# Gate rows spread by DMA, GpSimd's aggregates behind VectorE's first, buffers and prologue order changed

## The reference

```
h    = gelu(gelu(cond @ W0 + b0) @ W1 + b1);  att = softmax(h @ W2 + b2)     # 32 x 8, once
aggw = sum_k att[t, k] * weight[k]  (128 x 128);  aggb = att[t] @ bias_k
y    = bf16(aggw @ x[t] + aggb)
qg, sg = quant(y * inv_gate);  qu, su = quant(y * inv_up)     # per row: scale = max|.| / 127, codes = round
gate = (qg @ w_gate.T) * sg * s_wgate;  up = (qu @ w_up.T) * su * s_wup      # 1024 columns
inter = bf16(clip(silu(gate) * up, -10, 10));  qi, si = quant(inter * inv_inter)
out[t] = x[t] + (qi @ w_down.T) * si * s_wdown
```

## Time and profile before

| | us |
|---|---|
| median of 3 runs | 838.83 (838.81 to 840.03) |
| the profiled execution | 838.61 |
| its span, first instruction to last | 836.8 |
| PE busy | 811.7 |
| DVE busy | 715.6 |
| ACT busy | 443.0 |
| POOL busy | 152.1 |

### The profile page before, as it was taken

The page is one execution under the profiler, slowest core; times in us unless marked ns, Lnnn a source line. Parts: engine busy times, 40 slices in busy tenths (PEclk is TensorE's granted clock), DMA queues, the critical chain, the costliest instruction groups (busy, mean ns, idle before and its releaser), DMA issues.

```text
span 836.8 us, 9194 instructions
## 1 busy us (share of the span) xinstructions
PE 811.7 (97%) x3531; PEld 365.9 (44%) x3531; DVE 715.6 (86%) x799; ACT 443.0 (53%) x379; POOL 152.1 (18%) x146
## 2 busy tenths in 40 slices
PE   7898969899999999999999999999999999999997
PEld 2344434344444444444444444444444444444443
DVE  5575847999888898888889988888898888889968
ACT  2767322566565555565555556555555565545541
POOL 5630002111222222012222210222221012222000
PEclk9999989999999999999999999999999999999999
DMA  9962534355445454444554544445454454554242
GB/s 272 216 149 51 101 101 169 104 159 160 113 151 164 139 164 139 117 140 120 164 160 142 141 136 139 113 151 163 139 162 141 119 132 127 164 157 145 89 113 101
DMA packets 157918, 117.72 MB, mean 141 GB/s; under 512 B 147497, under 2 KB 147625, under 8 KB 148274
## 3 DMA queue, kind: packets, MB, share of 16 engines
q1 hardware_dynamic: 156146, 104.55, 41.4%
q0 software_dynamic: 1728, 12.58, 7.5%
HBM read 59.44 MB, written 33.55 MB: 111 GB/s over the span
## 4 chain that ended last, share of the span: by engine, by line
PE 88%; DVE 6%; ACT 2%; DMA 2%; issue 1%; DVEq 0%; ACTq 0%
PE up_ps L506 24%; PE gate_ps L506 24%; PE down_ps L580 24%; PE conv_ps L453 13%; DVE amax L875 1%; DMA wd<-w_downT 1%; DMA qgT<-qg 1%; PE down_ps L423 1%; DVE region L965 1%; DVE region L971 1%; ACT qg L686 0%; PE up_ps L423 0%; DVE region L981 0%; PE gate_ps L580 0%; PE conv_ps L415 0%
## 5 line engine op out<-in xcount | busy, mean ns | idle before, releaser
L506 PE MATMUL gate_ps<-wg,qgT 128*128 128x512 bf16 x992 | 219.7, 379 | 1.6 <-ACT qgT L730 1.6
L580 PE MATMUL down_ps<-wd,qiT 128*128 128x512 bf16 x912 | 214.8, 379 | 2.1 <-ACT qiT L766 2.1
L506 PE MATMUL up_ps<-wu,quT 128*128 128x512 bf16 x960 | 216.7, 379 | 0.0
L875 DVE TENSOR_REDUCE amax<-region 128x1 f32<-128x2048 f32 (+1 forms) x93 | 178.8, 1923 | 1.3
L357 POOL TENSOR_TENSOR prod<-wexp,att_bc 128x1024 f32<-128x1024 f32 x31 | 58.9, 1901 | 541.6 <-DVE region L915 516.6
L506 PEld LDWEIGHTS gate_ps<-wg,qgT 128*128 128x128 bf16 x992 | 96.9, 98 | 119.4 <-ACT qgT L730 2.1
L580 PEld LDWEIGHTS down_ps<-wd,qiT 128*128 128x128 bf16 x912 | 89.1, 98 | 128.0 <-issue 30.0
L506 PEld LDWEIGHTS up_ps<-wu,quT 128*128 128x128 bf16 x960 | 93.8, 98 | 113.5 <-issue 0.6
L453 PE MATMUL conv_ps<-xt,aggw 128*128 128x512 f32 x256 | 124.7, 612 | 6.1 <-issue 2.9
L686 ACT ACTIVATE qg<-region,recip 128x2048 f16<-128x2048 f32 x30 | 60.1, 2002 | 125.9 <-DVE recip L885 125.9
L677 ACT ACTIVATE y<-conv_ps,aggb 128x512 bf16<-128x512 f32 x120 | 81.8, 686 | 75.4 <-PE conv_ps L453 70.7
(11 more groups left out here) (124 smaller groups left out, 509.3 us busy)
## 6 DMA issues: line engine op xcount, KB each, us to landing
xt<-x SPq DMA_DIRECT2D x32, 1024.0 KB, 4.8
out<-xt SPq DMA_DIRECT2D x31, 1024.0 KB, 4.0
wg<-w_gateT POOLq DMA_DIRECT2D x4, 1024.0 KB, 19.0
wu<-w_upT POOLq DMA_DIRECT2D x4, 1024.0 KB, 19.5
wd<-w_downT POOLq DMA_DIRECT2D x4, 1024.0 KB, 7.7
out<-xt SPq DMA_DIRECT2D x4, 256.0 KB, 2.7
wexp<-weightT SPq DMA_DIRECT2D x1, 512.0 KB, 3.8
qgT<-qg SPq DMA_TRANSPOSE x28, 3.7
```

What stands on the lines that cost most here:

```text
L506: last = nc.tensor.matmul(acc[:, n * BANK:(n + 1) * BANK], codes[:, k * P:(k + 1) * P], wts[:, k, n * BANK:(n + 1) * BANK], start=(k == 0) ...
L580: last = nc.tensor.matmul(down_bank(t, c), qiT_at(t)[:, k * P:(k + 1) * P], wd[:, k, c * BANK:(c + 1) * BANK], start=(k == 0), stop=(k == ...
L875: nc.vector.tensor_reduce(amax[:, i:i + 1], src, axis=AX.X, op=ALU.max, apply_absolute_value=True).then_inc(max_ready, 1)
```

## The change

It does six things.
- inv_gate, inv_up and s_gate come as three inputs, and SP loads each with one DMA that reads the row 128 times, straight into invg_bc, invu_bc and swg_bc. inv_gate stands between x(0) and x(1); the other two follow the late rows, behind a wait for w_gate's third chunk, and x(3) follows them. All `spread` matmuls on TensorE, their ScalarE copies and the `warm` matmuls go.
- GpSimd waits for `agg_step` K (all of VectorE's aggregate of tile 0) before its own first aggregate.
- The scaled gate of tile 1 moves from w_down's part 5 to `prod`; the qiT buffers of tiles 0 and 1 move from `prod` to `qg`. GpSimd's wait for down(1) goes; ScalarE's `quant_g(4)` gets it. `gate_out(1)` waits for the aggregate of tile 4.
- TensorE: turn_u(0) stands before the first half of gate(2), not after it.
- ScalarE: quant_g(1) before conv_out(2); turned_g(2) and turned_u(0) earlier; quant_g(3) before silu(2); quant_u(3) from before turned_g(3) to after turned_i(2).
- VectorE: quant_g(3) before gate_out(2); quant_u(3) from before inner(1) to after inner(2).

```diff
-        GATE_HOME = [down_sc2[:, :], wd_part(5, fp32), wd_part(6, fp32)]
+        GATE_HOME = [down_sc2[:, :], prod[:, :, :].rearrange("p k o -> p (k o)"), wd_part(6, fp32)]
...
-        prod_bf = prod[:, :, :].rearrange("p k o -> p (k o)").bitcast(bf16)
-        QIT_HOME = [prod_bf[:, 0:KI * P], prod_bf[:, KI * P:2 * KI * P]]
+        qg_bf = qg[:, :].bitcast(bf16)
+        QIT_HOME = [qg_bf[:, 0:KI * P], qg_bf[:, KI * P:2 * KI * P]]
...
-            sp.dma_start(invg_s[0], rows[:, 0:I]).then_inc(rows_in[0], 16)
             sp.dma_start(wexp[:, :, :], weightT).then_inc(wexp_in, 16)
-            sp.dma_start(invg_s[1], rows[:, I:2 * I]).then_inc(rows_in[1], 16)
             sp.dma_start(xslot(0), x[0, :, :]).then_inc(x_in[0], 16)
+            sp.dma_start(invg_bc[:, :], inv_gate.partition_broadcast(P)).then_inc(rows_in[INVG], 16)
             sp.dma_start(xslot(1), x[1, :, :]).then_inc(x_in[1], 16)
-            for i, home in enumerate((invu_s[0], invu_s[1], swg_s)):
-                sp.dma_start(home, rows[:, (2 + i) * I:(3 + i) * I]).then_inc(rows_in[2 + i], 16)
             sp.dma_start(xslot(2), x[2, :, :]).then_inc(x_in[2], 16)
             for i, home in enumerate((swu_s, invi_s, swd_s[0], swd_s[1])):
                 sp.dma_start(home, late_rows[:, i * I:(i + 1) * I]).then_inc(late_in[i], 16)
+            sp.wait_ge(wg_in[2], 16)
+            sp.dma_start(invu_bc[:, :], inv_up.partition_broadcast(P)).then_inc(rows_in[INVU], 16)
+            sp.dma_start(swg_bc[:, :], s_gate.partition_broadcast(P)).then_inc(rows_in[SWG], 16)
             sp.wait_ge(gcodes_ready, 2)
...
-            pool.wait_ge(att_dve, ATT - 1)
+            pool.wait_ge(agg_step, K)
             aggregate(1)
...
-            pool.wait_ge(down_done, NC * 2)
...
-            pe.wait_ge(ones_set, 1)
-            warm(9)
             pe.wait_ge(mlp_in, 16)
+            pe.wait_ge(ones_set, 1)
...
-            for u in range(4):
-                spread(u)
-                warm(1)
             conv(0)
-            spread(4)
-            spread(5)
             conv(1)
             turn_g(0)
             conv(2)
             gate(0, HALVES[0])
-            spread(6)
-            spread(7)
             turn_g(1)
             gate(0, HALVES[1])
-            spread(8)
-            spread(9)
             gate(1, HALVES[0])
             turn_g(2)
             gate(1, HALVES[1])
+            turn_u(0)
             gate(2, HALVES[0])
-            turn_u(0)
             conv(3)
...
+                elif t == EARLY + 1:
+                    act.wait_ge(down_done, NC * 2)
...
-            for u in range(4):
-                spread_copy(u)
             conv_out(0)
-            spread_copy(4)
-            spread_copy(5)
             conv_out(1)
             quant_g_first()
             turned_g(0)
+            quant_g(1)
             conv_out(2)
-            quant_g(1)
-            spread_copy(6)
-            spread_copy(7)
             turned_g(1)
             quant_g(2)
-            spread_copy(8)
-            spread_copy(9)
+            turned_g(2)
             quant_u(0)
-            turned_g(2)
+            turned_u(0)
             silu(0)
-            turned_u(0)
             quant_u(1)
             conv_out(3)
             silu(1)
             turned_u(1)
             quant_u(2)
+            quant_g(3)
             silu(2)
-            quant_g(3)
             turned_u(2)
             quant_i(0)
-            quant_u(3)
             turned_g(3)
             turned_i(0)
             quant_i(1)
             turned_i(1)
             quant_i(2)
             turned_i(2)
+            quant_u(3)
             turned_u(3)
...
+                if t == 1:
+                    dve.wait_ge(agg_ready, 4)
...
             quant_u(2)
+            quant_g(3)
             gate_out(2)
-            quant_g(3)
             inner(0)
-            quant_u(3)
             inner(1)
             inner(2)
+            quant_u(3)
```

More of the change, by code:

```diff
@@ L3, with adaln_ffn @@
 from contextlib import ExitStack
-def adaln_ffn(nc, x, mlp, b2, weightT, w_gateT, w_upT, w_downT, rows, late_rows, out):
+def adaln_ffn(nc, x, mlp, b2, weightT, w_gateT, w_upT, w_downT, inv_gate, inv_up, s_gate, late_rows, out):
     fp32 = mybir.dt.float32
@@ L117, in adaln_ffn @@
         qiT16 = qiT[:, :].bitcast(fp16)
-        invg_s = wd_part(0, fp32)[0:1, :], wd_part(1, fp32)[0:1, :]
-        invu_s = wd_part(2, fp32)[0:1, :], wd_part(3, fp32)[0:1, :]
-        swg_s = wd_part(5, fp32)[0:1, :]
         swu_s = quT[0:1, :].bitcast(fp32)
@@ L137, in adaln_ffn @@
         ones = qiT[:, 0:2 * P].bitcast(fp32)
-        warm_s = qiT[:, 0:2 * P]
         logits = region2[:, 768:768 + B * K]
@@ L161, in adaln_ffn @@
         log_ps = up_ps[:, 0:B * K]
-        warm_ps = conv_ps[:, BANK:BANK + 2 * P]
         gturn_ps = down_ps[:, :].bitcast(fp16)
@@ L168, in adaln_ffn @@
         wexp_in = sem("wexp_in")
-        rows_in = [sem(f"rows_in{i}") for i in range(5)]
+        rows_in = [sem(f"rows_in{i}") for i in range(3)]
         late_in = [sem(f"late_in{i}") for i in range(4)]
@@ L182, in adaln_ffn @@
         ident_set = sem("ident_set")
-        spread_mm = sem("spread_mm")
-        spread_out = sem("spread_out")
         gturn_mm = sem("gturn_mm")
@@ L237, in adaln_ffn @@
         result_ready = sem("result_ready")
-        INVG, INVU, SWG = 4, 8, 10
+        INVG, INVU, SWG = range(3)
         SWU, INVI, SWD = 1, 2, 4
@@ L250, in adaln_ffn @@
         last_turn_ps = [bank(up_ps, h).bitcast(fp16)[:, 0:BANK] for h in range(2)]
[L252 to L257, removed]
         def gate_acc(t):
@@ L411, in _ @@
         def _(pe):
[L413 to L424, removed]
+            pe.wait_ge(mlp_in, 16)
             pe.wait_ge(ones_set, 1)
-            warm(9)
-            pe.wait_ge(mlp_in, 16)
             nc.tensor.matmul(hid_ps, w0_s, embT_s, start=True, stop=True).then_inc(hid_mm, 1)
-            warm(1)
             pe.wait_ge(hid_act, 1)
             nc.tensor.matmul(hid_ps, w1_s, h1, start=True, stop=True).then_inc(hid_mm, 1)
-            warm(3)
             pe.wait_ge(att_dve, 1)
@@ L444, in conv @@
                 for c in cs:
-                    if t == 0 and c < 2:
-                        pe.wait_ge(spread_out, 3)
-                    elif t == 3 and c < 2:
+                    if t == 3 and c < 2:
                         pe.wait_ge(uturn_out, c + 1)
@@ L450, in conv @@
                         pe.wait_ge(uturn_out, 9 + c)
-                    else:
+                    elif t > 0 or c >= 2:
                         pe.wait_ge(y_ready, NC * t + c - 1)
@@ L464, in turn_g @@
                     pe.wait_ge(gcodes_half, 1)
-                    pe.wait_ge(spread_out, 6)
                 else:
@@ L513, in gate @@
                         pe.wait_ge(qgT_ready, t - EARLY)
[L514 to L518, removed]
+                    if t == 2:
                         pe.wait_ge(gateval_ready, 1)
@@ L521, in gate @@
                         pe.wait_ge(upval_ready, 2)
-                    else:
+                    elif t > EARLY:
                         pe.wait_ge(gateval_ready, t)
@@ L659, in _ @@
         def _(act):
-            def spread_copy(u):
-                act.wait_ge(spread_mm, u + 1)
-                nc.scalar.activation(SPREAD_INTO[u], SPREAD_BANK[u], ACT.Copy).then_inc(spread_out, 1)
             def conv_out(t, cs=range(NC)):
@@ L720, in turned_i @@
                 if t == 0:
-                    act.wait_ge(agg_ready, 4)
+                    act.wait_ge(gturn_mm, GTURN["g", EARLY] + 2)
                     act.wait_ge(gturn_mm, GTURN["i", 0] + 1)
@@ L890, in quant_g @@
                     dve.wait_ge(gcodes_ready, t - 1 if t == 2 else t)
-                elif t == 1:
-                    dve.wait_ge(spread_out, INVG)
                 if t == EARLY + 1:
@@ L902, in quant_u @@
                 if t == 0:
-                    dve.wait_ge(spread_out, INVU)
+                    dve.wait_ge(rows_in[INVU], 16)
                 nc.vector.tensor_tensor(region2[:, :], y_at(t), invu_bc[:, :], ALU.mult).then_inc(xu_ready, 1)
@@ L926, in quant_first @@
                     dve.wait_ge(y_ready, c + 1)
-                    dve.wait_ge(spread_out, c + 1)
+                    if c == 0:
+                        dve.wait_ge(rows_in[INVG], 16)
                     scaled = nc.vector.tensor_tensor(region1[:, cols], y[:, cols], invg_bc[:, cols], ALU.mult)
@@ L945, in gate_out @@
                 if t == 0:
-                    dve.wait_ge(spread_out, SWG)
+                    dve.wait_ge(rows_in[SWG], 16)
+                if t == 1:
+                    dve.wait_ge(agg_ready, 4)
                 if t == 2:
@@ L1117 @@
         "w_gateT": blocked(L0_ffn_w_gate), "w_upT": blocked(L0_ffn_w_up), "w_downT": blocked(L0_ffn_w_down),
-        "rows": np.concatenate([np.asarray(L0_ffn_inv_gate), np.asarray(L0_ffn_inv_up),
-                                np.asarray(L0_ffn_s_wgate)]).reshape(1, -1),
```

(1 more changed line is left out.)

## The result

831.82 us median (831.34 to 832.92, 4 runs) against 838.82 before (4 runs): ratio 0.9918, 95% interval 0.9904 to 0.9931. That is 7.0 us faster where 12.0 were forecast (826.8); the time is inside the whole range of 821.5 to 834, and just outside the 823 to 831 that the main forecast had for itself. The profiled execution took 831.34, its span 829.5, 7.3 less than before.

A forecast was written before the change was run, and what follows sets the result against it. TensorE, busy 811.7 of 836.8 us, was taken to bound the kernel. Reaching down(1) 12.9 us sooner, less 0.9 for half clock, gave 12.0: 838.83 - 12.0 = 826.8 us, range 821.5 to 834.

The forecast's parts named there:

- the main forecast: Whole kernel: 12.0 us faster, 826.8 us, its own range 823 to 831; chance 0.60.
- rival 2: Row spreads by DMA 3 to 8 us slower at x(1) or invu_bc: gain 4 to 9, 832 us; chance 0.14.
- aggregate(0) and conv(0): Start: VectorE's steps cost 0.34 us without GpSimd; aggregate(0) done at 12.7, conv(0) starts at 12.75, 6.3 us sooner.
- Given back at quant_first: quant_first's multiplies wait beside GpSimd's aggregates: scale of tile 0 at 24.7 instead of 21.9, bounds 22 and 26.
- x(1) in x(2)'s place: SP's queue: the invg_bc spread ahead of x(1) takes an x tile's time, so x(1) lands at 20.2 instead of 11.3.
- rival 3: Row read 128 times at a third of the rate or less: slower, 843 us if invu_bc lands at 60; chance 0.08.
- First gate half, gate(2), up(1): TensorE's start: these begin at 35.3, 52.0 and 72.8, up(1) 9.5 us sooner; invu_bc and x(3) just in time.
- Rival 4: aggregate(0): VectorE's steps slow in themselves, 1.24 us each, so GpSimd merely starts later: 830 us; chance 0.02.
- The last down chunk: down(0): inner(2) at 88.2, fourth chunk lands at 99.0, TensorE there at 96.7: stall 2.3 us in place of 5.72.
- What is late next: Before turn_u(3): TensorE idles 3.0 us for ScalarE's quant_u(3), now 0.67; down(1) starts at 109.1 instead of 121.8.
- The clock: Half clock after two short idles close together around down(0) and turn_u(3): 0.9 us taken, bounds none and 2.0.
- The warm-up matmuls at nothing: Start: without the 17 matmuls conv(0)'s last two chunks could stay at half clock, 1.5 us, hidden by quant_first.

The follow-up runs named there:

- e4_no_pool_wait: Changed kernel with GpSimd's first aggregates released by att_bc again, as in the kernel before: 838.96 us, ratio to before 1.0004.
- e3_rows_early: Changed kernel without SP's wait for w_gate's third chunk, invu_bc and swg_bc issued right behind the late rows: 832.28 us, ratio to before 0.9928.
- e1_qu3_swap: Changed kernel with quant_u(3) before turned_i(2) again on ScalarE, VectorE's order kept: 828.93 us, ratio to before 0.9888.
- e2_clock_filler: Changed kernel with dummy matmuls in two TensorE idles, before the last down-weight chunk and before turn_u(3): 829.43 us, ratio to before 0.9902.
- e8_swap_and_split: Changed kernel with quant_u(3) before turned_i(2) on ScalarE and w_down's last chunk in two DMAs: 826.26 us, ratio to before 0.9849.
- a0_after_again: Changed kernel as it is, timed once more: 832.69 us, ratio to before 0.9930.

## Why the prediction was half right

The mechanism of the start came as forecast; the price of what is late behind it was too low. The time is inside the range, in part by luck: 831.8 is what rival 2 had (832), and its mechanism, slow row spreads, isn't there.

- *aggregate(0) and conv(0)*: forecast 12.7 and 12.75, came 12.9 and 13.15. The steps cost 0.35 for 0.34. So GpSimd was what slowed them; e4_no_pool_wait brings the 8.6 us back.
- *Given back at quant_first*: the scale of tile 0 was forecast at 24.7, came at 24.1. The bounds held, and so did the mechanism, VectorE waiting out GpSimd's step.
- *x(1) in x(2)'s place*: forecast 20.2, landed at 3.06 + 15.8 = 18.9. The row spread from HBM landed in 8.8 us, like an x tile, and invu_bc in 11.2 for the forecast's 10.9, which ends rivals 2 and 3.
- *First gate half, gate(2), up(1)*: forecast 35.3, 52.0, 72.8; came 33.5, 50.25, 71.97. invu_bc was there at 41.7 for a forecast of 41.9, x(3) at 55.7 for 55.2. That they don't set the pace by more than about 1 us is shown by e3_rows_early. Rival 4 is refuted by the 352 ns.
- *The last down chunk*: a step that was partly wrong. I let inner(2) follow inner(1)'s codes at 88.2. But quant_i(1) stands on ScalarE behind turned_i(0), which needs TensorE's turn_i(0), which stands behind up(2): inner(2) came at 89.58, the chunk at 100.1 for 99.0, and TensorE was there 0.8 us sooner than I had it. Stall 4.19 for 2.3, 1.9 more.
- *What is late next*: forecast a 3.0 us idle for quant_u(3) on ScalarE; came 3.01. e1_qu3_swap takes it away.
- *The clock*: the term that was mis-sized. I took 0.9 us with a bound of 2.0, the loss of the kernel before, as a difference on top of full clock. Measured: 2.66 in down(0) (8.26 less 5.6), 0.7 in the turn, 1.0 in down(1), 4.4 in all, and e2_clock_filler gives 4.2 of it back. The bound was for one idle; here were two, each followed by its own stretch at half clock, and the 0.9 was a choice between bounds and not worked out. In the six profiles with both idles the same loss is 3.3 to 4.7 us.
- *The shortfall*: up(1) to up(3) was forecast at 43.8 (72.8 to 128.6 less 12.0) and took 49.3. 3.5 us of clock and 1.9 of the longer stall make 5.4 of these 5.5. Up(1) came 0.8 sooner than forecast, so 4.7 are left: 7.3 by the spans for 12.0. The median's 5.0 has 0.3 more. The prediction also has 12.9 where its own 121.8 less 109.1 gives 12.7.
- *No loss between 130 and 200 us*: right, 708.2 us in both.
- *The warm-up matmuls at nothing*: not tested by itself; the slow first chunks of conv(0) weren't always hidden, as said above.

The Trainium skill (SBUF — State Buffer, "SBUF: two separate sides") says that whoever of the shared pair starts first has it for the whole instruction, and that the other is blocked. The runs agree that one of the two waits: 352 ns a step without GpSimd, a median of 1300 beside it, and a multiply of 2.27 or 5.47 us. On who is first they don't follow the recorded starts: the multiply of 5.47 began 1.37 us ahead of GpSimd's step, during GpSimd's issue of loads.

## What to carry to other kernels

When a wait is moved off the path, price the clock behind every idle that is left, once for each, and not once for all: here two idles of 3 to 4 us cost 4.4 us beyond themselves, and idles of 0.7 to 1.7 us cost nothing in e8_swap_and_split. An operation that goes later on one engine (quant_u(3) on VectorE) must be followed through the in-order queue of the next (ScalarE behind turned_i(2)); one swapped pair there was worth 3 to 4 us. A profile is one execution: here four of ten had up(1) some 4 us later, so compare a stretch that doesn't hold the disturbed place. Two edits may be worth little or nothing alone and 7 us together, so take each away from the whole and also try it alone.

## What was not expected of the hardware

The DMA that spreads one 8 KB row over 128 partitions landed in 8.8 us behind an x tile and at the pace of one; nothing showed that reading one place 128 times costs more. A VectorE multiply took 2.27 or 5.0 to 5.5 us, and what told the two apart in ten profiles was whether it began 0.16 us after GpSimd's issue of three loads or 0.29 and more: a tenth of a microsecond decides on 3. It showed as some 3.5 us in up(1)'s start (76.03 in a0_after_again for 72.50 in e3_rows_early, both with conv(2)'s later half at half clock, 3.78 and 3.68 us).
